# Transformer block on one core: features loaded by unit of four heads behind the maxima transfers, the rope moved around the split of the maxima, and row fills and bias loads moved at the start

## The reference

```python
x = x + 0.5 * ffn(layernorm(x), weight, bias, delta_w, delta_act)
x = x + attention(layernorm(x), wq, bq, wk, bk, wv, bv)
x = x + 0.5 * ffn(layernorm(x), weight, bias, delta_w, delta_act)

def attention(x):                      # per batch, 16 heads of 8 columns
    q, k, v = x @ wq.T + bq, x @ wk.T + bk, x @ wv.T + bv
    q, k = rope(q), rope(k)
    return softmax(q @ k.T / sqrt(8)) @ v
def ffn(x):                            # mxfp4: blocks of 32 columns, a power-of-two scale each
    return quant(x) @ quant(weight).T + bias
```

## Time and profile before

| | |
|---|---|
| runs | 588.16, 591.27, 600.82 us; median 591.27 |
| profiled execution | 590.53 us; first to last instruction 588.5 us |
| mean granted TensorE clock | 0.947 of full speed |
| busy | PE 487.7, DVE 438.6, ACT 398.7, POOL 230.9 us |
| DMA | 30.81 MB in 22590 packets |

### The profile page before, as it was taken

One profiled execution on the slowest core, in us unless ns is written; L12 is line 12 of the kernel. 1 busy time (PEld: TensorE's weight loads), 2 busy tenths in 40 slices (PEclk: granted clock), 3 DMA queues, 4 the chain that ended last, 5 costly groups with the idle time before them and its releaser, 6 DMA issues.

```text
span 588.5 us, 10108 instructions
## 1 busy us (share of the span) xinstructions
PE 487.7 (83%) x2662; PEld 171.2 (29%) x2662; DVE 438.6 (75%) x1020; ACT 398.7 (68%) x766; POOL 230.9 (39%) x350
## 2 busy tenths in 40 slices
PE   1261879899899998999889888999899997998861
PEld 0121223332233333333223233333233322322211
DVE  6346979785989689967968597867996686889215
ACT  4816158686868787778748685778777774778740
POOL 4401173326544455446432544346442713012300
PEclk9996599999999999999979999999999997999995
DMA  3305304500350027001600034001600161000000
GB/s 83 94 9 138 67 11 109 100 2 11 99 109 20 3 57 159 8 17 46 161 14 20 11 99 109 15 5 51 161 6 19 33 155 31 20 1 2 19 1 18
DMA packets 22590, 30.81 MB, mean 52 GB/s; under 512 B 4998, under 2 KB 20236, under 8 KB 20236
## 3 DMA queue, kind: packets, MB, share of 16 engines
q1 hardware_dynamic: 20908, 29.87, 21.0%
q10 hardware_dynamic: 1632, 0.39, 0.3%
HBM read 21.47 MB, written 8.39 MB: 51 GB/s over the span
## 4 chain that ended last, share of the span: by engine, by line
PE 52%; issue 11%; DVE 10%; DMA 9%; POOL 9%; ACT 5%; SPq 2%; POOLq 1%; DVEq 0%; ACTq 0%
PE ot L1104 15%; PE sc L1091 13%; PE st L1080 11%; DMA feat_q<-maxrows 8%; DVE negmax L878 4%; POOL qkpre L457 3%; PE misc L1027 2%; PE misc L1069 2%; ACT probs L632 2%; PE misc L1044 2%; PE misc L1052 1%; ACT feat_k L522 1%; DVE stats_f L746 1%; DMA feat_k<-parts_k 1%; PE misc L1061 1%
## 5 line engine op out<-in xcount | busy, mean ns | idle before, releaser
L878 DVE TENSOR_REDUCE negmax<-sc 128x1 f32<-128x512 f32 x512 | 333.0, 682 | 88.7 <-PE sc L1091 88.2
L632 ACT ACTIVATE probs<-st 128x512 f32<-128x512 f32 x512 | 272.4, 599 | 89.0 <-PE st L1080 87.9
L1091 PE MATMUL sc<-feat_k,feat_q 96*128 96x512 bf16 x512 | 190.4, 397 | 10.2 <-DVE negmax L878 9.1
L1080 PE MATMUL st<-feat_q,feat_k 99*128 99x512 bf16 x512 | 157.1, 384 | 16.9 <-DMA feat_q<-maxrows 10.6
L1104 PE MATMUL ot<-probs,vfeat 128*32 128x512 f32 x1024 | 139.6, 618 | 1.0 <-ACT probs L632 1.0
L1091 PEld LDWEIGHTS sc<-feat_k,feat_q 96*128 96x128 bf16 x512 | 49.9, 98 | 167.3 <-DVE negmax L878 117.0
L1080 PEld LDWEIGHTS st<-feat_q,feat_k 99*128 99x128 bf16 x512 | 49.6, 99 | 87.6 <-ACT probs L632 43.8
L457 POOL TENSOR_TENSOR qkpre<-qkpre,ropeT 128x512 f32<-128x512 f32 x28 | 35.6, 1271 | 45.7 <-ACT qkpre L581 45.7
L442 POOL TENSOR_SCALAR maxparts<-negmax 128x16 bf16<-128x16 f32 x32 | 8.2, 257 | 90.6 <-DVE negmax L878 90.6
L1044 PE MATMUL misc<-xnT,wqkT 128*128 128x512 f32 x56 | 30.8, 633 | 2.7 <-DVE onorm L895 2.0
L481 POOL TENSOR_TENSOR xres<-xres,onorm 128x128 f32 (+1 forms) x31 | 14.1, 453 | 46.9 <-DVE onorm L895 46.9
(11 more groups left out here) (132 smaller groups left out, 471.6 us busy)
## 6 DMA issues: line engine op xcount, KB each, us to landing
feat_q<-parts_q SPq DMA_DIRECT2D x48, 192.0 KB
feat_k<-parts_k SPq DMA_DIRECT2D x48, 192.0 KB
parts_q<-qkparts_q SPq DMA_DIRECT2D x24, 128.0 KB, 2.3
parts_k<-qkparts_k SPq DMA_DIRECT2D x24, 128.0 KB, 2.3
xres<-in_L_attn_x_dram SPq DMA_DIRECT2D x8, 256.0 KB, 4.8
out_dram<-xres SPq DMA_DIRECT2D x8, 256.0 KB, 2.3
feat_q<-maxrows ACTq DMA_DIRECT2D x32, 12.0 KB
wload<-in_L_ffn_weight_dram SPq DMA_DIRECT2D x1, 64.0 KB, 2.4
```

The lines of the kernel that those rows point to most:

```text
L632: nc.scalar.activation(probs[:, s % US, j * S:(j + 1) * S], st[:, bank(2 * s + j), :], ACT.Exp, scale=SCALE).then_inc(exp_done, 1)
L878: nc.vector.tensor_reduce(negmax[:, g, j:j + 1], sc[:, bank(16 * g + j), :], AX.X, ALU.max, negate=True).then_inc(sc_maxed, 1)
L1080: nc.tensor.matmul(st[:, bank(2 * s + j), :], feat["k"][par][0:MROWS, h, kb * P:(kb + 1) * P], feat["q"][par][0:MROWS, h, :], start=True, ...
L1091: nc.tensor.matmul(sc[:, bank(16 * g + j), :], feat["q"][par][0:SROWS, h, t * P:(t + 1) * P], feat["k"][par][0:SROWS, h, :], start=True, s ...
```

## The change

- The due steps of the projection of the swapped keys, of the rope of the keys and of the parts that follow are later. POOL now has the split of the maxima (step 33) ahead of both key products (33, 34), where the second product and the sum stood ahead of it (32).
- The features are loaded by unit: four groups of six DMAs of 96 KB, with a semaphore each. The first two groups are issued at step 44, behind a wait for the maxima load of unit 2 of the batch before; the other two at step 52, behind the one of unit 3. `scores` waits at each unit's start for its own group.
- The two bias vectors are loaded right behind the identity, on a semaphore of their own with it, and POOL's bias steps wait for that one alone.
- Three row fills on ACT move back: two from `set_up` to behind the first `copy_xqT`, one from there to behind the first `copy_xnT`.

```diff
-PROJ = dict(stats=20, rstd=21, norm=23, turn=25, qk=(27, 29, 30, 31), rope=(28, 30, 31, 32), high=(32, 34),
-            rest=(34, 35), mid=(35, 36), low=(36, 37), write=37, load=40, v=35)
+PROJ = dict(stats=20, rstd=21, norm=23, turn=25, qk=(27, 29, 31, 32), rope=(28, 30, 33, 34), high=(32, 37),
+            rest=(35, 38), mid=(36, 39), low=(38, 40), write=40, load=(44, 52), v=35)
...
-        feat_loaded = [sem(f"feat_loaded{half}") for half in range(2)]
+        feat_loaded = [sem(f"feat_loaded{g}") for g in range(G)]
...
-            sp.dma_start(ident[:, :], ident_in).then_inc(consts_loaded, 16)
+            sp.dma_start(ident[:, :], ident_in).then_inc(bias_loaded, 16)
+            for i, src in enumerate((bv, bias)):
+                sp.dma_start(biasin[:, i * D:(i + 1) * D], src.partition_broadcast(PARTS)).then_inc(bias_loaded, 16)
...
-            for i, src in enumerate((bv, bias)):
-                sp.dma_start(biasin[:, i * D:(i + 1) * D], src.partition_broadcast(PARTS)).then_inc(consts_loaded, 16)
...
-            def load_features(b, par):
-
-                if after(2 * STEPS * (b - 1)):
-                    sp.wait_ge(st_ready, 2 * STEPS * (b - 1))
-                if known(b) and b < 2:
-                    sp.wait_ge(init_act, ACT_STEPS - 3 + 3 * b)
-                sp.wait_ge(parts_out, 96 * (b + 1))
-                for half in range(2):
-                    heads = slice(H // 2 * half, H // 2 * (half + 1))
+            def load_features(b, par, half):
+
+                if half == 0:
+                    if known(b) and b < 2:
+                        sp.wait_ge(init_act, ACT_STEPS - 3 + 3 * b)
+                if after(32 * b):
+                    sp.wait_ge(max_loaded[half], 32 * b)
+                if half == 0:
+                    sp.wait_ge(parts_out, 96 * (b + 1))
+                for g in (2 * half, 2 * half + 1):
+                    heads = slice(UH * g, UH * (g + 1))
...
-                feature_rows("q", 0, 0)
-                feature_rows("k", 0, 1)
...
                             if known(nb) and (n, nb) == ("f1", 0):
-                                feature_rows("q", 1, 0)
+                                feature_rows("q", 0, 0)
+                                feature_rows("k", 0, 1)
                     for nb, _ in turns_of_batch(b, par, s, PROJ["turn"], 2):
                         copy_xnT(nb)
+                        if known(nb) and nb == 0:
+                            feature_rows("q", 1, 0)
...
-                if j == 0 and g % 2 == 0:
-                    pe.wait_ge(feat_loaded[g // 2], FEATS * (b + 1))
+                if j == 0:
+                    pe.wait_ge(feat_loaded[g], FEATS * (b + 1))
```

More of the change, by code:

```diff
@@ L157, in macaron_kernel @@
         w_loaded = sem("w_loaded")
+        bias_loaded = sem("bias_loaded")
         consts_loaded = sem("consts_loaded")
@@ L204, in macaron_kernel @@
                  (("pe", nc.tensor), ("act", nc.scalar), ("dve", nc.vector), ("pool", nc.gpsimd))}
-        CONSTS = 17 * 16
+        CONSTS = 14 * 16
+        BIASES = 3 * 16
         FEATS = 2 * PARTS * 16
@@ L305, in write_parts @@
                 if after(FEATS * b):
-                    for half in range(2):
-                        sp.wait_ge(feat_loaded[half], FEATS * b)
+                    for g in range(G):
+                        sp.wait_ge(feat_loaded[g], FEATS * b)
                 for a in range(PARTS):
@@ L331, in load_features @@
                         sp.dma_start(feat["q"][par][c:PROD:PARTS, heads, :].rearrange("r h s -> r (h s)"),
-                                     q).then_inc(feat_loaded[half], 16)
+                                     q).then_inc(feat_loaded[g], 16)
                         sp.dma_start(feat["k"][par][PARTS * HD * c:PARTS * HD * (c + 1), heads, :]
-                                     .rearrange("r h s -> r (h s)"), k).then_inc(feat_loaded[half], 16)
+                                     .rearrange("r h s -> r (h s)"), k).then_inc(feat_loaded[g], 16)
             def store(b):
@@ L344, in slot @@
                         write_parts(nb, npar)
-                    for nb, npar in turns_of_batch(b, par, s, PROJ["load"], 2):
-                        load_features(nb, npar)
+                    for half in range(2):
+                        for nb, npar in turns_of_batch(b, par, s, PROJ["load"][half], 2):
+                            load_features(nb, npar, half)
                     for nb, npar in turns_of_batch(b, par, s, FFN2["store"], -1):
@@ L378, in set_up @@
             def set_up():
-                pool.wait_ge(consts_loaded, CONSTS)
+                pool.wait_ge(bias_loaded, BIASES)
                 link(nc.gpsimd.tensor_scalar(biasin[:, D:2 * D], biasin[:, D:2 * D], 0.5, None, ALU.mult))
@@ L534, in set_up @@
             def set_up():
+                act.wait_ge(bias_loaded, BIASES)
                 act.wait_ge(consts_loaded, CONSTS)
@@ L984, in _ @@
         def _(pe):
+            pe.wait_ge(bias_loaded, BIASES)
             pe.wait_ge(consts_loaded, CONSTS)
@@ L1109, in slot @@
             def slot(b, par):
-                before = (qk_pre, 4 * b + 4)
+                before = (qk_pre, 4 * b + 3)
                 if known(b) and b == 1:
-                    assert last[0] == before, "the slot before is to end with the swapped keys"
+                    assert last[0] == before, "the slot before is to end with the keys"
                 if not known(b) or b == 6:
```

## The result

The changed kernel ran at 561.69, 563.14, 565.32 and 568.19 us, a median of 564.23; beside it on the same chip the kernel before had a median of 590.87. The ratio is 0.957 (95% interval 0.9505 to 0.9634): faster. The forecast was 562 us with a range of 555 to 575. The profiled execution is the 568.19 one, 4 us above its own median; the experiments showed why that matters.

What follows compares the result with a forecast made beforehand. The prediction took PE to set the pace, losing most in waits for the maxima load and its split. 18.0 + 7.5 + 4.9 - 1.5 = 28.9 us off 590.5 gave 561.6, forecast as 562 us, range 555 to 575.

Steps and rivals of the forecast that it cites:

- Where the pace is set: PE sets the pace, busy 57.3 of 61.5 us in batch 2; waits for maxima load (10.6) and split (12.7) explain most loss.
- Step 1: Third unit of batches: feature loads placed behind the maxima loads remove the collision that makes PE wait; 18.0 us off.
- the rival that it isn't there: Third unit: feature loads don't delay the maxima load, so 18.0 us of lateness stays; 580 us, chance 0.05.
- The Trainium skill's rule of queues served in turn: DMA engines alternate queues packet by packet, so the maxima load waits for about one packet and pacing gains nothing there.
- The first group: Step 49's plain scores: six loads land 5.8 us after first issue, 2.8 us early; cost nothing. Late: 569 us, chance 0.13.
- Step 2: Second unit of six batches: rope no longer delays POOL's split of the maxima; 7.5 us off, less 1.5 for moved work.
- The 1.5 us for what is moved beside step 40: Cost, 0.2 us a batch, of moved projection products, ACT copy and POOL's low part of the keys.
- The rival's 7 us: Around step 40 ACT and POOL get crowded and give back 1.25 us a batch; 569 us, chance 0.16.
- Step 3: The start: later row fills and earlier biases, less later due steps, bring the first plain scores to 54.3; 4.9 us off.
- The lower clock: Start: clock 0.50 from 48 to 75 us; if it stays as it is, the start gains only 2 us.
- All between 60 and 61.5 us, with clock 1.00: Sign of success: the length of every batch window and its granted clock after the change.
- a clock that falls for another reason: Sign that the prediction is wrong: the granted clock falls for a cause other than those it named.

Runs made afterwards that it cites:

- third group: Four kernels on one chip beside the kernel before: negated mean by tensor_reduce with and without pacing, 559.32 and 559.79 us; old start, 575.29; changed kernel unedited, 571.55.
- e1_loads_only: The kernel before with the feature loads alone changed, by unit and behind the maxima loads; 577.02 us, ratio 0.9671.
- e9_nm_reduce: The changed kernel with a layer norm's negated mean on VectorE made by a negated tensor_reduce instead of a tensor_scalar; 559.32 us, ratio 0.9459.
- e2_due_steps_only: The kernel before with only the due steps of projection, rope and parts changed, loads by half at step 41, not paced; 576.22 us, ratio 0.962.
- e11_old_start: The changed kernel with the old start: constants behind one semaphore, biases last, all row fills in ACT's set-up; 575.29 us, ratio 0.9745.
- two-input form: The changed kernel with the negated mean made by a tensor_tensor (zero minus mean) instead of a tensor_scalar; 569.28 us, ratio 0.9647.

## Why the prediction was right, and where it wasn't

**The total.** 562 predicted, 564.23 measured, inside the range. Part of that is luck: the same kernel had 571.55 us on the chip of the third group, still inside, and without the stretch 559.32. The sum was made for a kernel without stretches.

**Where the pace is set.** Right. In `e1_loads_only` 10.6 us of PE's waits went, and its profile is 15.5 us shorter (575.08 against 590.53, on different chips): more than the waits, since the clock no longer fell in batches 1 and 3.

**Step 1, 18.0 us.** The size is about right: 19.4 us in `e1_loads_only` by the ratio, 15.5 between the profiles. By batches the terms were 1.55, 1.7, 4.8, 4.1 and 5.8 us for batches 0, 1, 3, 4 and 6, and the windows of `e1_loads_only` gave 1.7, 1.9, 4.8, 0.8 and 5.0. The term of batch 4 failed: the clock fell there without the load's wait too. Only together with the other parts does that batch come to 61.66 us at a clock of 1.00 (`e9_nm_reduce`). The collision is real, and the rival that it isn't there is refuted: with nothing but the loads changed, its waits go. The Trainium skill's rule of queues served in turn ("DMA: Bandwidth & Descriptors", section "Queues, rings and completion order") is not refuted by the count of 283 against 1: that window begins before the load's issue, and the rule's packet is a group of descriptors, which the trace's packets (51 for 12 KB) need not be. What speaks against a wait of one packet is that the wait grew with what was issued ahead: the first packet came 2.5 us after the issue with two loads of 192 KB ahead, 5.2 us with seven (`e2_due_steps_only`, batches 0 and 2), and 7.0 us with eleven (kernel before, batch 6). What failed is the attribution: "SP now starts a batch's loads only when that maxima load has landed" is what the prediction priced, and it is dispensable (564.05 us without it, and 559.79 against 559.32). Loads by unit, which it gave nothing of their own, keep the maxima load clear without pacing, and their first group lands after 6 us where that of a half takes 9.6.

**The terms overlap.** The prediction added steps 1 and 2 as if they were apart. Alone, by their ratios on 590.87 us, they are worth 19.4 and 22.5 us, and the start another 5.7: 48 in all, where the whole change has 25.4 by its ratio, or 32 with the reduce (0.9459). The intervals of the first two are 8 and 10 us to either side, so it is again the traces that show it: either change alone takes PE's 10.6 us of waits for the maxima load down to 0.2 or nothing. The sum still came out near, because step 2 was priced by the split's wait alone and not by what it does to the loads.

**The first group.** The wait of six loads was priced at 5.8 us behind the issue, 54.1 - 48.3. SP's first issue at 47.60 is followed by plain scores at 53.80 with no wait, so it took 6.2 at most. "I take nothing" was right.

**Step 2, 7.5 us less 1.5.** The gain is right: the split's waits fell by 7.9 us (12.7 to 4.8). The 1.5 us for what is moved beside step 40 was mis-sized, and not by crowding: the rival asked whether POOL is too busy (it isn't, 9.6 of 14.8 us). What counts is which DVE instruction starts together with POOL's, and the lines of the kernel before had a case of it (L778 beside L431, above). The price is 0.9 to 3.1 us for each stretch, in none to five batches: 9.1 us between the profiles of the changed kernel (568.19) and the reduce (559.13), which ran on different chips, and 12.2 us between medians on one chip. The rival's 7 us had the right place and about the right size for the wrong cause, which is luck.

**Step 3, 4.9 us.** Right: 5.8 us in `e11_old_start`, and the plain scores were predicted at 54.3 and came at 53.80. The 5.0 us that the new due steps take there are in `e2_due_steps_only`, 4.8. The lower clock moved along with the work and kept its length: 27.3 us from 47.9 before, 27.3 us from 41.8 in the changed kernel.

**The windows.** "All between 60 and 61.5 us, with clock 1.00" failed in batches 3 to 5, and the text named the reading for it, a clock that falls for another reason. With the reduce batches 1 to 4 are 60.04, 60.15, 60.55 and 61.66 us at 1.00: the sum was that of this kernel.

## What to carry to other kernels

Here a small DMA on one queue stood behind what another queue had piled up. Making the large ones so small that each was about moved when the next was issued, with a semaphore for each piece, did as much as waits that order them, so try it first. Before moving a step of GpSimd, look at which VectorE instruction will start beside it: a tensor_scalar of four numbers paid for a whole GpSimd instruction, and its tensor_reduce form didn't. Where runs of one kernel spread by over 1%, profile it more than once: two profiles of the changed kernel showed three stretches and five, and one of its two-input form none.

## What the runs showed that I had not expected

- VectorE's 128x4 tensor_scalar and tensor_tensor took 1.14 to 1.16 us instead of 0.16 when GpSimd's 128x512 tensor_tensor started 19 to 28 ns ahead of them, but not every time: where GpSimd's started 16 to 21 ns ahead they also ran in 0.16 us, and GpSimd's took 0.04 us more. tensor_reduce took 0.15 us at the same place, 23 to 27 ns behind.
- One late 0.16 us instruction a batch cost up to 3.1 us: PE idled for 1.34 us, then the granted clock stood at 0.50 (1.2 GHz) for some 6.8 us in which PE was busy for 6.4. In other batches the same stretch left the clock at 1.00 and cost 1.0 us.
- The same kernel had a median of 564.23 us on one chip and of 571.55 on another. Its profiles had three and five stretches. That the number of stretches makes the difference between the other runs as well fits the 2.5 us spread without them, but only profiled runs show it.
